# Spare tiles' weights: copied by SyncE, or read in place by TensorE; and one mask chunk on GpSimd

## What is computed

```python
x = x + tanh(g_xattn[0]) * softmax_attention(layernorm(x), ctx, ...)
x = x + tanh(g_ffn[0]) * masked_experts(layernorm(x), weight, scale, expert_masks, router_w)
x = x + tanh(g_xattn[1]) * sparse_adjacency(ctx, layernorm(x), Wq, Wk, gamma_raw)   # top 76 of 256 per row
x = x + tanh(g_ffn[1]) * gated_experts(layernorm(x), gate_w, gu_w, dp_w, ...)        # 64 experts, top 8

# masked_experts: each row goes to its one best expert of 32
top1_idx = argmax(softmax(x @ router_w.T)); top1_w = max(softmax(...))
w_q = clip(round(weight / 0.5), -1, 1)                  # ternary
y[row] = x[row] @ (w_q * scale * expert_masks[top1_idx[row]]).T * top1_w[row]
```

## Time and profile before

| | |
|---|---|
| median of 3 runs | 405.51 us (404.76 to 406.37) |
| the profiled execution's own time | 406.02 us |
| its span, first to last instruction | 404.3 us |
| TensorE products busy | 358.7 us (89% of the span) |
| VectorE busy | 272.6 us (67%) |
| ScalarE busy | 181.1 us (45%) |
| GpSimd busy | 163.0 us (40%) |
| mean granted TensorE clock | 0.947 of full |
| moved by transfers | 51.31 MB, 127 GB/s |

### The profile page before, as it was taken

The page is one execution under the profiler, slowest core; times in us unless marked ns, Lnnn a source line. Parts: engine busy times, 40 slices in busy tenths (PEclk is TensorE's granted clock), DMA queues, the critical chain, the costliest instruction groups (busy, mean ns, idle before and its releaser), DMA issues. The chain is left out here.

```text
span 404.3 us, 7694 instructions
## 1 busy us (share of the span) xinstructions
PE 358.7 (89%) x2419; PEld 217.4 (54%) x2419; DVE 272.6 (67%) x711; ACT 181.1 (45%) x354; POOL 163.0 (40%) x180
## 2 busy tenths in 40 slices
PE   8987928643977899999899999969999999999995
PEld 2755426312644365546466666645665656656563
DVE  3999896999376585999784484557555555555454
ACT  3477736624744446544645446533323233332331
POOL 6937542437551349978699677220000000000000
PEclk9996967785999899999999999999999999999999
DMA  7899964686701444445355442004121221212211
GB/s 186 139 258 218 197 208 149 221 263 217 233 17 51 128 137 131 130 131 195 132 190 174 159 153 73 25 29 146 61 78 58 72 71 58 78 56 74 77 53 52
DMA packets 50346, 51.31 MB, mean 127 GB/s; under 512 B 6732, under 2 KB 41484, under 8 KB 50318
## 3 DMA queue, kind: packets, MB, share of 16 engines
q1 hardware_dynamic: 34430, 38.08, 30.0%
q0 software_dynamic: 9216, 6.29, 9.1%
q10 hardware_dynamic: 6672, 6.59, 5.1%
HBM read 44.13 MB, written 7.08 MB: 127 GB/s over the span
## 5 line engine op out<-in xcount | busy, mean ns | idle before, releaser
L1047 PE MATMUL bank<-early,gu 128*128 128x512 f16 x768 | 177.7, 381 | 3.0 <-DVE arena L1608 3.0
L1047 PEld LDWEIGHTS bank<-early,gu 128*128 128x128 f16 (+1 forms) x768 | 75.0, 98 | 83.0 <-issue 4.4
L499 ACT ACTIVATE arena<-arena 128x512 f16<-128x512 f32 (+1 forms) x66 | 41.6, 631 | 134.6 <-DVE arena L1624 133.8
L1074 PE MATMUL bank<-dp,arena 128*128 128x256 f16 (+1 forms) x768 | 94.2, 273 | 1.1 <-POOL arena L457 0.7
L1074 PEld LDWEIGHTS bank<-dp,arena 128*128 128x128 f16 x768 | 74.7, 98 | 23.5 <-POOL arena L457 2.7
L1608 DVE TENSOR_TENSOR arena<-arena,bank 128x512 f32<-128x512 f32 x64 | 43.9, 686 | 56.7 <-PE bank L1047 40.2
L457 POOL TENSOR_TENSOR arena<-arena 128x512 f16<-128x512 f32 (+1 forms) x33 | 38.3, 1161 | 51.1 <-ACT arena L499 51.1
L1624 DVE TENSOR_TENSOR arena<-arena,early 128x512 f32<-128x512 f32 x64 | 48.4, 756 | 7.5 <-DVE arena L1608 2.7
L740 ACT ACTIVATE arena<-bank 128x512 f32<-128x512 f32 (+1 forms) x66 | 38.7, 588 | 17.5 <-PE bank L1047 17.4
L406 POOL TENSOR_TENSOR gu<-stage,gu 128x512 f16<-128x512 f32 x32 | 39.0, 1219 | 7.4 <-ACT dp L499 7.4
L1634 DVE TENSOR_TENSOR arena<-arena 128x512 f16<-128x512 f32 (+1 forms) x33 | 22.8, 691 | 24.5 <-ACT arena L499 24.5
(11 more groups left out here) (184 smaller groups left out, 368.6 us busy)
## 6 DMA issues: line engine op xcount, KB each, us to landing
early<-token_weights SPq DMA_DIRECT2D x126, 128.0 KB, 2.9
stage<-in_gu_t SPq DMA_DIRECT2D x32, 256.0 KB
gu<-in_masks_t POOLq DMA_DIRECT2D x16, 256.0 KB, 22.5
stage<-in_dp_t SPq DMA_DIRECT2D x32, 128.0 KB
expert_rows<-arena ACTq DMA_DIRECT2D x12, 256.0 KB
dp<-gu SPq DMA_DIRECT2D x22, 128.0 KB, 2.3
routed_rows<-arena SPq DMA_DIRECT2D x1, 1536.0 KB, 17.5
arena<-routed_rows ACTq DMA_DIRECT2D x3, 512.0 KB, 5.1
```

The costliest lines, as they stand in the source:

```text
L499: return nc.scalar.activation(dst, src, ACT.Copy, scale=scale)
L1047: last = mm(dst[:, :], w, x16[:, h, b, c, :], start=(k == 0), stop=(k == 3 * C - 1))
L1074: last = mm(dst, inter16[0:m, s, a, k * P:(k + 1) * P], w, start=(q is None and j == 0 and k % 2 == 0), stop=True, skip_group_check=True)
```

## The change

- **Spare tiles in place.** SyncE's copies (`load_spares`, `wov`) are gone. TensorE loads the 15 owners' numbers of a half into registers (`spare_owners`) and addresses `m16` by them. The routed rows of spare tiles are copied into `spare_x` (in `dp16`, zeroed once by VectorE), where each tile's 32 columns lie between zeros, so that a product over the full width adds four tiles with different weights into one result: 32 products of full width per piece.
- **Last mask chunk.** GpSimd multiplies chunk 7 after `rsqrt(3)`; VectorE does chunks 0 to 6.
- **Order.** On TensorE `ranks(0)` comes before `sim1(1)`, and the logits of half 1 before half 0's experts; the fillers are distributed anew. On VectorE `attend(1)` comes before the masks. On ScalarE `softmax_rows(1)`, `router_rows(1)` and `norm_rows(1)` come before half 0's experts; `load_rows(1)` and `tanh_rows(0)` after `store_rows(0, 3)`; `router_exp(1)` after `store_rows(0, 5)`; the weighing goes between half 1's experts, and that of tiles 4 to 7 ahead of the second layer. On GpSimd `rsqrt(4)` comes before `low_half(4)`, `gather(1)` right after that, and `add_rows` of tiles 4 to 7 before the second layer's loop. On VectorE the last searches of half 0 move behind `rows_affine(0)`.

```diff
@@ -73,7 +73,11 @@
         xT = gu16[:, 4:16, :, :, :].rearrange("p a b c d -> p (a b c d)").rearrange(
             "p (h k c s n) -> p h k c s n", h=2, k=ROWS, c=C, s=2)
 
+
         dp16 = sb("dp16", [P, PAIRS, 2, D], F16)
+        spare_zero = dp16[:, PAIRS // 2:, :, :].rearrange("p a b c -> p (a b c)")
+        spare_x = spare_zero.rearrange("p (k c s n) -> p k c s n", k=4, c=C, s=2)
+        own_x = spare_zero.rearrange("p (a j n) -> p a j n", j=4, n=P)[:, :, :, 0:CAP]
 
...
@@ -275,15 +275,6 @@
                     sp.wait_ge(lo_ready, q - 1)
                 sp.dma_start(stage_gu[s], gu_d[:, :, q, :]).then_inc(stage_in[s], 16)
                 sp.dma_start(stage_dn[s], dp_d[:, q, :]).then_inc(stage_in[s], 16)
-
-            def load_spares(h):
-
-                sp.wait_ge(owner_set, h + 1)
-                sp.wait_ge(mask_ready, MB)
-                for j in range(SPARE):
-                    e = sp.value_load(spare_e[0:1, h, j:j + 1], min_val=0, max_val=E0 - 1)
...
@@ -309,11 +300,7 @@
             load_row(scale_sb[:, :], scale0, late_in)
             load_pair(2)
             load_pair(3)
-            load_spares(0)
-            load_pair(4)
-            load_pair(5)
-            load_spares(1)
-            for q in range(6, 8):
+            for q in range(4, 8):
                 load_pair(q)
 
...
@@ -467,6 +454,12 @@
             low_half(2)
             low_half(3)
             rsqrt(3, HT)
+            pool.wait_ge(tern_set, 1)
+            pool.wait_ge(mask_in[MB - 1], 16 * C)
+            for c in range(C):
+                w = m16[:, ME * (MB - 1):, c, :]
+                last = nc.gpsimd.tensor_tensor(w, w, tern16[:, c, None, :].to_broadcast([P, ME, D]), ALU.mult)
+            last.then_inc(last_masks, 1)
             for t in range(HT, T):
                 low_rows(t)
             scatter(1)
@@ -474,20 +467,21 @@
             pool.wait_ge(late_in, 16 * 4)
             for t in range(HT):
                 add_rows(t)
-            for q in range(4, 7):
-                low_half(q)
             rsqrt(4, HT)
+            low_half(4)
+            gather(1)
+            low_half(5)
+            low_half(6)
+            rsqrt(5, HT)
             low_half(7)
-            rsqrt(5, HT)
-            gather(1)
+            for t in range(HT, T):
+                add_rows(t)
             low_step(0, 1, I1)
             low_step(1, 0)
             for n in range(2, NS):
                 low_step(n, (n + 1) % 2)
-                if n == 10:
+                if n == 8:
                     rsqrt(6, HT)
-                if 4 <= n < 4 + HT:
-                    add_rows(n)
                 if 4 <= n < PAIRS - 4:
                     low_half(n + 4)
...
@@ -615,9 +609,22 @@
                     act.dma_start(xs16[h][:, 4 * j:4 * j + 4, :], rows_v[:, 4 * j:4 * j + 4, :]
                                   ).then_inc(xs_in[h][j], 16)
 
+            def spare_rows(h, p):
+
+                if h == 0:
+                    act.wait_ge(spare_set, 1)
+                else:
+                    act.wait_ge(y_ready, p + 1)
+                a = 4 * C * (p - E0 // 8)
+                copy(own_x[:, a:a + 4 * C, :, :], ps_xt[p % 2].rearrange("p (a j n) -> p a j n", j=4, n=CAP)
+                     ).then_inc(xt_copied, 1)
+
             def routed_rows(h, p):
 
...
@@ -647,13 +654,14 @@
             high_half(1)
             norm_rows(0, 0, 1, 2, 3)
             scale_rows(1)
+            router_exp(0)
+            softmax_rows(1)
             sim1_rows(1, 0, 1)
-            router_exp(0)
             high_half(2)
-            tanh_rows(0)
             high_half(3)
             load_rows(0)
-            softmax_rows(1)
+            router_rows(1)
+            norm_rows(1, 4, 5, 6, 7)
             routed_rows(0, 0)
             routed_rows(0, 1)
             expert_rows(0, 0)
@@ -662,20 +670,19 @@
             expert_rows(0, 1)
             routed_rows(0, 3)
             store_rows(0, 1)
-            router_rows(1)
-            norm_rows(1, 4, 5)
             expert_rows(0, 2)
             routed_rows(0, 4)
             store_rows(0, 2)
-            norm_rows(1, 6, 7)
             expert_rows(0, 3)
             routed_rows(0, 5)
             store_rows(0, 3)
-            router_exp(1)
+            load_rows(1)
+            tanh_rows(0)
             expert_rows(0, 4)
             store_rows(0, 4)
             expert_rows(0, 5)
             store_rows(0, 5)
+            router_exp(1)
 
             def weigh_rows(*tiles):
 
...
@@ -684,9 +691,6 @@
                     copy(Z[:, t, :], Z[:, t, :], wtop[:, t:t + 1]).then_inc(zw_ready, 1)
 
             high_half(4)
-            high_half(5)
-            load_rows(1)
-            weigh_rows(0, 1, 2, 3)
             routed_rows(1, 0)
             routed_rows(1, 1)
             expert_rows(1, 0)
...
@@ -695,19 +699,23 @@
             expert_rows(1, 1)
             routed_rows(1, 3)
             store_rows(1, 1)
+            weigh_rows(0, 1)
             expert_rows(1, 2)
             routed_rows(1, 4)
             store_rows(1, 2)
+            weigh_rows(2, 3)
             expert_rows(1, 3)
             routed_rows(1, 5)
             store_rows(1, 3)
-            high_half(6)
             expert_rows(1, 4)
             store_rows(1, 4)
             expert_rows(1, 5)
             store_rows(1, 5)
+            high_half(5)
+            high_half(6)
             mix_rows(0)
             high_half(7)
+            weigh_rows(4, 5, 6, 7)
 
             def prep_rows(h):
 
...
@@ -935,6 +939,27 @@
                 pe.wait_ge(started_ready, h + 1)
                 mm(ps_owner, ones16[0:E0, 0:E0], started16[:, :], start=True, stop=True).then_inc(owner_ready, 1)
 
+            owner = []
+
+            def spare_owners(h):
+
+                pe.wait_ge(owner_set, h + 1)
+                owner[:] = [pe.value_load(spare_e[0:1, h, j:j + 1], min_val=0, max_val=E0 - 1) for j in range(SPARE)]
+
+            def experts_spare(h, p):
+
+                n = PIECES * h + p
+                pe.wait_ge(xt_copied, n + 1)
+                for k in range(2):
+                    first = 2 * p + k - E0 // 4
+                    for i in range(8 * C):
+                        j, c, s = i // (2 * C), i // 2 % C, i % 2
+                        e = owner[min(4 * first + j, SPARE - 1)]
+                        last = mm(ps_y[p % 2][:, k * D:(k + 1) * D], spare_x[:, first, c, s, 96 * j:96 * j + P],
+                                  m16[:, bass.ds(e, 1), c, :].rearrange("p e o -> p (e o)"),
+                                  start=(i == 0), stop=(i == 8 * C - 1))
...
@@ -956,24 +981,25 @@
             def experts(h, p, *ks):
 
                 n = PIECES * h + p
-                pe.wait_ge(mask_ready, min(2 * p + 2, MB))
+                pe.wait_ge(mask_ready, min(2 * p + 2, MB - 1))
+                if p == PIECES // 2:
+                    pe.wait_ge(last_masks, 1)
                 if n < 2:
                     pe.wait_ge(proj_copied, 6)
                     pe.wait_ge(router_set, 1)
                     pe.wait_ge(xnt_copied, 2)
                 else:
                     pe.wait_ge(y_copied, n - 1)
-                if p == E0 // 8:
-                    pe.wait_ge(wov_in[h], 16 * SPARE)
+                if p >= E0 // 8:
+                    experts_spare(h, p)
+                    return
                 pe.wait_ge(xt_copied, n + 1)
                 for k in ks or (0, 1):
                     for i in range(2 * C):
                         c, s = i // 2, i % 2
                         for j in range(4):
-                            e = 4 * (2 * p + k) + j
-                            w = m16[:, e, c, :] if e < E0 else wov[h][min(e - E0, SPARE - 1)][:, c, :]
                             last = mm(ps_y[p % 2][CAP * j:CAP * (j + 1), k * D:(k + 1) * D],
-                                      xT[:, h, 2 * p + k, c, s, CAP * j:CAP * (j + 1)], w,
+                                      xT[:, h, 2 * p + k, c, s, CAP * j:CAP * (j + 1)], m16[:, 4 * (2 * p + k) + j, c, :],
                                       start=(i == 0), stop=(i == 2 * C - 1), skip_group_check=True)
                 if k == 1:
                     last.then_inc(y_ready, 1)
...
@@ -1102,33 +1128,35 @@
             keep_busy(8, bank[0][:, :])
             router_x((0, 1))
             router(0)
-            sim1(1, 0, 1)
-            keep_busy(4, bank[0][:, :])
+            keep_busy(8, bank[0][:, :])
             ranks(0)
             keep_busy(2, bank[0][:, :])
             owners(0)
             keep_busy(2, bank[0][:, :])
             owners_of(0)
-            keep_busy(36, bank[0][:, :])
+            sim1(1, 0, 1)
+            spare_owners(0)
+            keep_busy(20, bank[0][:, :])
+            router_x((2, 3))
+            keep_busy(4, bank[0][:, :])
+            router(1)
+            keep_busy(4, bank[0][:, :])
             routed_x(0, 0)
             routed_x(0, 1)
             experts(0, 0)
             routed_x(0, 2)
+            ranks(1)
```

(37 more changed lines are left out.)

31 lines of the change are left out of this document (13 added, 18 removed).

## The result

The changed kernel took 415.87 us in the median of four runs (414.05 to 420.23), the kernel before 405.94 beside it: ratio 1.026 (95% interval 1.018 to 1.035). In a second measurement, on another chip, it took 414.72 (413.47 to 415.99) against 409.67: 1.012 (1.008 to 1.016). The kernel before, timed against itself once, gave 0.994. So the change costs 5 to 10 us, and a ratio here moves by 0.6% with the occasion.

A forecast was written before the change was run, and what follows sets the result against it. Bound: TensorE's second feed-forward layer, so its start time counts. VectorE's wait for router_exp(1) and a longer tail put it off 6.9 us, the layer itself gives -1.0: +5.9, so 411.4 us, range 406.8 to 417.5.

The forecast's parts named there:

- Register loads: On TensorE's queue, 15 owner loads per half at 0.59 us each (bounds 0.42 and 0.74), 8.8 us a half.
- the third rival, cheap loads: TensorE's register loads take 0.3 us or less, with no clash; 407.5 us, chance 0.13.
- Spare pieces: On TensorE, each full-width piece of 32 products takes 3.5 us (up to 5.4) against 1.06 before.
- GpSimd's chunk: GpSimd's two mask products of 1024 elements take up to 2.3 us each, 4.4 together.
- The clash: VectorE's remaining mask chunks may wait for GpSimd's: done at about 64.5 at worst, 58 without; logits come later.
- The course: Stage times before the layer: logits 65.3, slots 73.9, load_rows(1) 80.6, exponential 87.3, last mask 118.4, layer start 130.3.
- In the layer: Inside the second feed-forward layer, GpSimd's additions and ScalarE's weighing leave the loop: -1.0 us, bounds -3 and +0.5.
- The reason given: VectorE's weighing waits 12 us for router_exp(1), queued behind load_rows(1) on ScalarE; the layer starts 6.9 us later.
- TensorE as the bound: Dearer loads or spare pieces use up TensorE's 3.4 us slack; 415.5 to 419 us, chance 0.16.
- The larger clash: GpSimd's mask products take 4 us each against VectorE's; choose(1) at 68.4, everything 4 later, 415.5 us, chance 0.12.
- Faster: Half 1's routing leads early, with loads at 0.1 and no clash; 403 us, chance 0.07.
- It does not do what it says: Addressing by register makes each TensorE product wait for its address; counted as the first rival, no separate chance.

The follow-up runs named there:

- e0: The changed kernel itself, unaltered, timed and profiled again: 414.72 us, ratio 1.012 to the kernel before.
- e7: Changed kernel with router_exp(1) and two weigh_rows moved earlier, 14 fillers behind symmetric(0, 1), constant owners replacing register loads: 413.21 us, ratio 1.011.
- e9: e8 with constant owners in place of the 30 register loads: 413.27 us, ratio 1.017 to the kernel before.
- e1: Changed kernel with only router_exp(1) moved ahead of load_rows(1) in ScalarE's queue: 414.45 us, ratio 1.010 to the kernel before.
- e3: Changed kernel with the last mask chunk multiplied by VectorE again instead of GpSimd: 414.48 us, ratio 1.011 to the kernel before.
- first profile: First profiled execution of the unaltered changed kernel: 420.23 us, the slowest of its four runs.
- e2: Changed kernel with constant owners in place of the 30 register loads: 417.97 us, ratio 1.021 to the kernel before.
- e5: Changed kernel with router_exp(1) behind store_rows(0, 1) and two weigh_rows around half 1's first routed_rows: 411.35 us, ratio 1.010 to the kernel before.
- e8: Changed kernel with router_exp(1), weigh_rows and tanh_rows(0) moved earlier, 14 fillers behind symmetric(0, 1): 411.73 us, ratio 1.013 to the kernel before.
- e11: e8 with gather(1) behind rsqrt(5), four weigh_rows behind ScalarE's copies, high_half(5) and (6) between expert copies: 407.10 us, ratio 1.003.

## Why the prediction was right, and where it was not

*The sum.* Forecast +5.9; e0's profile against the earlier trace rows gives 131.11 - 123.42 = +7.7 at the layer start (forecast +6.9) and +0.5 in the rest (forecast -1.0): +8.2 of span. Taken by medians the two measurements gave +9.9 and +5.1. Right in sign and range, 2.3 us short in the profile. VectorE's terms add up to 31.2 from 87.3, so 118.5 and not 118.4, and GpSimd's two products of up to 2.3 to 4.6 and not 4.4; neither moves the result.

*Register loads,* taken at 0.59: from 47.2 to 57.1 there are 15, so 0.66 each, 9.9 a half; between the bounds, by 1.1 us a half too low. A record is 0.30 and its arithmetic 0.15; the remaining 0.2 is no record but SEQ_ASSERT's 0.02. The Trainium skill (DMA: Bandwidth & Descriptors, Latency and other measured facts) gives a floor of about 600 ns that unrolling in fours amortizes: the period agrees with it, the record alone is half of it, and 15 loads on end amortized nothing. So the third rival, cheap loads, is out.

*Spare pieces,* 3.5: 7.15 / 2 = 3.57. Right, with nothing added for addressing by register: with constants (e7, e9) 64 products took 7.15 too. What the forecast did not have is a stop in e0, e1 and e3, where half 0's two pieces took 9.7 us:

```profile
78.62 0.82 PE L958 MATMUL bank<-gu,dp 128*128 x6 [0.88 <-issue]
79.97 3.66 PE L958 MATMUL bank<-gu,dp 128*128 x32 [0.53 <-ACT dp L493]
```

Those are e0's; ScalarE stood still there for 3.70 us. The profile names no instruction of the core as its releaser, and no run shows the cause. It took 2.6 us of TensorE's slack.

*GpSimd's chunk,* at most 2.3 a product: 2.29 and 2.57. *The clash:* two VectorE products beside them took 2.60 instead of 0.68, and in e0 `choose(1)` came out of the masks at 64.5, the forecast's upper bound, 0.2 us behind the logits. The Trainium skill (GPSIMD Engine Reference, Specifications) says the two share their SBUF interfaces; this trace agrees, and e3 shows that it cost no time.

*Zeroing* took 3.47 us and hid behind the load of X, as forecast.

*The course,* forecast and e0: logits done 65.3 and 64.3; slots 73.9 and 72.6; `load_rows(1)` 80.6 and 79.2; exponential done 87.3 and 86.7; VectorE's stop 12 and 12.73; last adjacency 118.4 and 118.3; `rows_mix` done 121.2 and 121.6. Errors within it cancelled: `owners_of(0)` ended 1.4 us later than forecast and `sim1(1)` ran at the low clock (3.47, not 2), but the fillers took 5.9, not 8.5. Behind `rows_mix` the tail was 131.1 - 121.6 = 9.5, where 8.2 + 0.8 was forecast. So of the 2.3 us, 0.4 arose up to `rows_mix` and 0.5 in the tail (in tenths, rounded); the other 1.5 is the term of the layer, next.

*In the layer,* -1.0: the waits did go. By lines behind the layer start, before and e0:

```profile
L1047 PE MATMUL bank<-early,gu 128*128 128x512 f16 x768 | 177.7, 381 | 3.0 <-DVE arena L1608 3.0
```

```profile
L1073 PE MATMUL bank<-early,gu 128*128 128x512 f16 x768 | 178.2, 382 | 0.1
```

That is 2.9 us, and 1.1 us of waits at `down` went as well. e0 gave it back. Its trace has two long stretches at the low clock behind the layer start, 13.6 us in all, where before's has 3.4 us at 133.0; at half speed the 10.2 us more can cost up to 5.1, as an estimate. That this is the cause is argued from these rows, and no run tried it:

```profile
138.60:145.40 6.80, 6.73 (x14) 2.00 (x13) 2.47 (x4) 4.18 (x6) 2.14 (x2) 0.51 0.43 139
271.80:278.60 6.80, 5.89 (x22) 3.57 (x23) 2.14 (x6) 1.22 (x2) 1.47 (x2) 0.50 0.14 41
```

In the first profile, without the second of them, the rest was 278.2, so -2.7 against before.

*The reason given,* VectorE's wait for `router_exp(1)`, was true as a description and too narrow as a cause. The prediction named one other path level with it, by `low_half(4)` and pair 6, and said TensorE had 3.4 us of slack. The runs showed more such paths: `tanh_rows(0)`, which I had counted as 2.1 us ahead of the exponential but not as something VectorE needs; `weigh_rows` behind TensorE's loads; `gather(1)` ahead of `rsqrt(5)` and pair 7. The step that failed was following each moved result to only one reader. It did not show in the time, because all were late by about the same. That the time came out right, although undoing the one wait it was built on (e1) wins nothing, is in part luck.

*The rivals.* TensorE as the bound: in e0 `symmetric(0, 1)` began right behind the 24 fillers, at 118.69, 0.4 us after the last adjacency, so the slack of 3.4 was in truth nearly 0: 2.6 of it went in the stop above and 1.1 in the loads of half 1. Taking the loads away won nothing in e2, where VectorE was as late, nor in e7 and e9, where ScalarE's copies covered them. So in e0 TensorE was level with VectorE and GpSimd, and not the bound by itself. The larger clash: ruled out by e3. Cheap loads: out, as above. Faster: no. "It does not do what it says": the spare pieces took their 7.15 us with registers and with constants.

## What to carry to other kernels

When a transfer that waits for data is moved up in an in-order queue, list every result queued behind it and every engine that reads one: freeing one of them alone (e1, e5, e8) handed the wait on to the next. And an undo that gains nothing does not clear its suspect: here no undo up to e8 gained more than the 0.6% by which ratios scatter, though e5's profile began its layer 3.5 us earlier, and the set of them (e11) brought back 6.3 of the 7.7 us at the layer start. Then mend the kernel before in the same way, or the set's gain is taken for proof that the rest of the change is free.

## What the runs showed of the hardware

- The granted clock differs between executions of one kernel: 10 us at 0.50 near the start in two profiles of the changed order (the first, e3), 6.7 us in two more, and none in the records of the others, with TensorE busy. The first and e3 had their logits of half 1 4.2 and 4.5 us after e0's. In e1 the products ran at half speed there while the record showed the full level.
- A VectorE product of two f16 inputs (1024 elements, 0.68 us alone) took 2.60 us beside a GpSimd product of 2.3 to 2.6 us, and not a mean of the two. `attend`'s f32 products (0.48 us alone), four in 3.96 us, were slow beside `low_half` pieces as well; so were products of one f32 tile and two scalars per row, four in 3.39 us against 1.38.
- A register load on TensorE's queue costs 0.66 us with its arithmetic, and the loads start while products already issued still run: 9.9 us of loads left 6.9 to 9.0 us of idle time in front of the fillers.
- Addressing the weights by register added nothing: 64 products of 256 columns took 7.15 us with registers and with constants.
